# Mixture-of-experts stage of a small language model: gathered rows turned by TensorE, inner product turned by DMA, down product three tiles behind

## The reference

```python
h = tok(x)                                   # softmax of 4 coefficients, times 4 base rows
h = h + attn(layernorm(h))                   # 16 heads, q = k = v
xn = layernorm(h)
topk_logits, topk_idx = top_k(xn @ moe_router, 2)            # 8 experts, 2 for each token
w = softmax(topk_logits)
# for each (token, expert) pair, pairs sorted by expert:
gate, up = split(xn[token] @ moe_w13[expert])                # 256 -> 2 x 512
hidden = silu(gate) * up                                     # 512
h = h + sum over a token's two experts of w * (hidden @ moe_w2[expert])   # 512 -> 256
```

## Time and profile before

| | |
|---|---|
| Median of three runs | 920.97 us (919.45 to 924.36) |
| Profiled execution, its own time | 920.03 us |
| Its span | 918.3 us |
| TensorE busy with matmuls (PE) | 780.5 us, 85% |
| VectorE / ScalarE / GpSimd busy | 532.2 / 547.2 / 357.3 us |
| Expert stage | from 596.5 us to the end |
| TensorE in that stage, from 640 to 700 us | 59.66 of 60 us, granted clock 1.00 |
| DMA engines there | busy half of the time |

### The profile page before, as it was taken

The page is one execution under the profiler, slowest core; times in us unless marked ns, Lnnn a source line. Parts: engine busy times, 40 slices in busy tenths (PEclk is TensorE's granted clock), DMA queues, the critical chain, the costliest instruction groups (busy, mean ns, idle before and its releaser), DMA issues. The chain is left out here.

```text
span 918.3 us, 17297 instructions
## 1 busy us (share of the span) xinstructions
PE 780.5 (85%) x5470; PEld 331.6 (36%) x5521; DVE 532.2 (58%) x1617; ACT 547.2 (60%) x512; POOL 357.3 (39%) x311
## 2 busy tenths in 40 slices
PE   3499995988899889988988893079999999999994
PEld 2132221222222222222222221036666666666662
DVE  6734573647776657585646467725555555555552
ACT  0368994999999999999999993112222222222221
POOL 7660030320432133223320345335656556665652
PEclk9999997999999999999999996579999999999997
DMA  1030104012101110111011204035544455554442
GB/s 38 1 90 2 35 12 35 13 44 61 47 13 36 47 47 13 58 47 47 14 36 46 70 26 133 18 73 88 96 92 84 93 91 90 87 97 86 87 71 30
DMA packets 71920, 50.38 MB, mean 55 GB/s; under 512 B 45382, under 2 KB 67544, under 8 KB 71854
## 3 DMA queue, kind: packets, MB, share of 16 engines
q1 hardware_dynamic: 55598, 32.02, 14.7%
q0 software_dynamic: 16256, 17.55, 11.4%
HBM read 22.79 MB, written 17.57 MB: 44 GB/s over the span
## 5 line engine op out<-in xcount | busy, mean ns | idle before, releaser
L701 ACT ACTIVATE shared<-PS 128x1536 f32<-128x1536 f32 x342 | 467.9, 1472 | 55.1 <-PE PS L335 44.9
L347 PE MATMUL PS<-shared,va 128*32 128x512 f32 x2048 | 277.8, 615 | 3.4 <-DVE room L1141 3.1
L586 POOL DMA_INDIRECT slots<-pair_no,room x64 | 63.5, 992 | 382.8 <-DVE room L827 368.2
L1361 PE MATMUL PS<-w_p,room 128*128 x793 | 190.1, 382 | 15.0 <-DMA room<-room 12.9
L335 PE MATMUL PS<-room,ak 32*128 32x512 bf16 x1024 | 131.5, 391 | 53.2 <-ACT shared L701 44.7
L1409 ACT ACTIVATE room<-PS 128x512 f32<-128x512 f32 x69 | 41.3, 598 | 162.7 <-PE PS L1361 162.7
L1331 POOL DMA_INDIRECT out<-room,idx_tok x68 | 107.5, 1581 | 77.4 <-ACT room L1414 65.0
L1461 DVE CAST room<-PS 128x512 bf16<-128x512 f32 x68 | 47.0, 692 | 126.5 <-PE PS L1370 126.5
L1361 PEld LDWEIGHTS PS<-w_p,room 128*128 128x128 f16 x828 | 81.3, 98 | 99.2 <-issue 18.0
L335 PEld LDWEIGHTS PS<-room,ak 32*128 32x128 bf16 x1024 | 31.7, 91 | 205.1 <-ACT shared L701 150.0
L1378 PE MATMUL PS<-shared,room 128*128 x828 | 101.8, 273 | 0.3 <-DVE room L1463 0.3
(11 more groups left out here) (260 smaller groups left out, 650.4 us busy)
## 6 DMA issues: line engine op xcount, KB each, us to landing
room<-w SPq DMA_DIRECT2D x24, 512.0 KB, 4.8
xrows<-room SPq DMA_DIRECT2D x16, 258.0 KB, 3.1
out<-room SPq DMA_DIRECT2D x16, 256.0 KB
room<-xrows,idx_tok POOLq DMA_INDIRECT x70, 2.9
room<-room SPq DMA_TRANSPOSE x70, 3.5
out<-room,idx_tok POOLq DMA_INDIRECT x68, 4.1
slots<-pair_no,room POOLq DMA_INDIRECT x64, 6.8
xT<-xT SPq DMA_DIRECT2D x3, 256.0 KB, 5.9
```

The costliest lines, as they stand in the source:

```text
L347: last = pe.matmul(PS[32 * slot:32 * slot + 32, ACC, :], g.va[:, KT * (grp // HG) + kt, c, :], prob[:, (4 * quad + slot) % (RING * WIDE), ...
L586: pool.indirect_dma_start(g.slots, bass.IndirectOffsetOnAxis(pos_i[:, grp % 2, 2 * k + kk:2 * k + kk + 1].bitcast(U32), 0), g.pair_no[:, t ...
L701: act.activation(prob[:, at:at + n, :].rearrange("p n q -> p (n q)"), PS[:, buf:buf + n, :].rearrange("p c q -> p (c q)"), ACT.Exp).then_i ...
L1361: last = pe.matmul(PS[:, up_bank(k) + half, :], xsT[:, k, 2 * a + c, :], g.w13_p[:, w, c, ds(e, 1), FF * half:FF * half + FF].rearrange("p ...
```

## The change

Only the expert block changes, and one constant for it (`identh`, a float16 identity, written by one more VectorE instruction at the very start).

- The gathered rows are turned by TensorE (`turn_x`): four float16 transposes of 128 x 128 into the first half of bank 0 or bank 5, and one copy by ScalarE to `xsT` (`copy_x`).
- The inner product `hid` isn't turned by TensorE. VectorE splits it in place into two bfloat16 halves, L1441 and L1443 (now from SBUF to SBUF), and SyncE issues one DMA transpose of 128 x 1024 values, eight blocks, straight to `hidT`, which has four buffers now.
- In TensorE's program a step is `turn_x` of tile j + 4, `up` of tile j + 3, `down` of tile j.
- `act_s` and `hid` have one buffer each; the loop's last iteration is written out, 68 tiles are gathered and multiplied, and no 69th.
- GpSimd scatters tile j - 7 behind the gather of tile j, where it was tile j - 6.

```diff
@@ sync
-            sp.wait_ge(xs_in[k], arrived)
-            sp.sem_inc(x_landed, 1)
-            sp.dma_start_transpose(xsT[:, k], xs[:, k, 0:4 * P]).then_inc(xT_in[k], 16)
+            sp.wait_ge(hid_split, j + 1)
+            sp.sem_inc(sp_step, 1)
+            sp.dma_start_transpose(hidT[:, k], halves[:, k].rearrange("p a f -> p (a f)")).then_inc(hT_in[k], 16)
@@ gpsimd
-            for j in range(XBUF, tiles + 2):
+            for j in range(XBUF, tiles):
                 pool.wait_ge(weighed, j - XBUF + 1)
                 pool.wait_ge(up_mm, j - XBUF + 1)
                 gather(j)
-                if j >= XBUF + 2:
-                    scatter(j - XBUF - 2, apart)
+                if j >= XBUF + 3:
+                    scatter(j - XBUF - 3, apart)
@@ tensor
+        def turn_x(k, j, round_):
+            pe.wait_ge(xs_in[k], 16 * round_ + 16)
+            pe.wait_ge(xT_copied, j + 1)
+            for c in range(4):
+                last = pe.transpose(PS[:, XB[k % 2], 0:2 * P].bitcast(F16)[:, P * c:P * c + P], xs[:, k, P * c:P * c + P], g.identh[:])
+            last.then_inc(x_turned, 1)
+
+        def up(k, j, round_):
+            e = expert(j)
+            pe.wait_ge(xT_copied, j + 1 + FREE)
+            pe.wait_ge(hid_ready, j + 1)
...
-        def turn_hidden(k, ready, free):
-            pe.wait_ge(hid_ready, ready)
-            pe.wait_ge(hidT_ready, free)
-            for c in range(4):
-                last = pe.transpose(PS[:, HTB, P * c:P * c + P], hid[:, k, P * c:P * c + P], g.ident[:])
-            last.then_inc(hid_turned, 1)
...
+        def down(k, j, round_):
+            e = expert(j)
+            pe.wait_ge(hT_in[k], 16 * round_ + 16)
+            pe.wait_ge(y_copied, j + 1)
...
-                up((k + 1) % XBUF, expert(j + 2), i * 16 + 16 * ((k + 1) // XBUF + 1), j + FREE)
-                turn_hidden(k % 2, j + 1 + FREE, j + FREE)
-                down((k + 1) % 2, expert(j), j + FREE, j - 1 + FREE)
+                if not last:
+                    turn_x(k, j + XBUF, i + 1)
+                if not last or k == 0:
+                    up((k + 3) % XBUF, j + 3, i + (k + 3) // XBUF)
+                down(k, j, i)
+
+        for j in range(XBUF):
+            turn_x(j, j, 0)
+            if j >= 1:
+                up(j - 1, j - 1, 0)
+        steps(pe, body)
@@ scalar
+        def copy_x(k, j):
+            act.wait_ge(x_turned, j + 1)
+            act.copy(xsT[:, k].rearrange("p c q -> p (c q)"), PS[:, XB[k % 2], 0:2 * P].bitcast(F16)).then_inc(xT_copied, 1)
...
+                if not last:
+                    copy_x(k, j + XBUF)
+                if not last or k == 0:
+                    silu((k + 3) % XBUF, j + 3)
+                copy_y(k, j)
@@ vector
+            dve.wait_ge(hid_ready, j + 1 + FREE)
+            dve.tensor_copy(halves[:, k, 0], hid[:]).then_inc(split_step, 1)
+            dve.wait_ge(split_step, j + 1)
+            dve.tensor_tensor(halves[:, k, 1], hid[:], halves[:, k, 0], ALU.subtract).then_inc(hid_split, 1)
```

More of the change, by code:

```diff
@@ L1281, in up_bank, with steps @@
+    y_mm, y_copied, y_free = sem("y_mm"), sem("y_copied"), sem("y_free")
+    weighed = sem("weighed")
+    x_turned, xT_copied = sem("x_turned"), sem("x_copied")
+    XB = (0, 5)
+    YB = (6, 7)
     def up_bank(k):
         return 1 + 2 * (k % 2)
-    def steps(eng, body, end):
+    def steps(eng, body):
         more = eng.value_load(g.more[0:1, 0:1], min_val=0, max_val=1)
-        with eng.Fori(0, USUAL // XBUF) as i:
-            body(i)
+        with eng.Fori(0, USUAL // XBUF - 1) as i:
+            body(i, False)
@@ L1302, in body, with turn_hidden @@
-        def body(i):
-            for k in range(XBUF):
[L1304 to L1311, removed]
+        def turn_hidden(k, j):
+            sp.wait_ge(hid_split, j + 1)
+            sp.sem_inc(sp_step, 1)
+            sp.dma_start_transpose(hidT[:, k], halves[:, k].rearrange("p a f -> p (a f)")).then_inc(hT_in[k], 16)
+        def body(i, last):
+            for k in range(XBUF):
+                turn_hidden(k, i * XBUF + k)
@@ L1340, in run @@
                 gather(j)
-                if j >= XBUF + 2:
-                    scatter(j - XBUF - 2, apart)
-            for m in range(tiles - XBUF, tiles):
+                if j >= XBUF + 3:
+                    scatter(j - XBUF - 3, apart)
+            for m in range(tiles - XBUF - 3, tiles):
                 scatter(m, apart)
@@ L1354, in tensor, with expert @@
     def tensor(pe):
[L1355 to L1357 removed]
+        def expert(j):
+            col = j + 1
+            return pe.value_load(g.tile_expert[0:1, ds(col, 1) if not isinstance(col, int) else slice(col, col + 1)],
+                                 min_val=0, max_val=E - 1)
+        def turn_x(k, j, round_):
[8 more added lines that the diff above has]
+            pe.wait_ge(hid_ready, j + 1)
             for half in range(2):
@@ L1381, in down, with body @@
             last.then_inc(y_mm, 1)
[L1383 to L1388, removed]
-        pe.sem_inc(y_mm, FREE)
-        pe.wait_ge(zeroed, 2)
-        up(0, expert(1), 16, FREE)
-        def body(i):
+        def body(i, last):
             for k in range(XBUF):
                 j = i * XBUF + k
-                up((k + 1) % XBUF, expert(j + 2), i * 16 + 16 * ((k + 1) // XBUF + 1), j + FREE)
-                turn_hidden(k % 2, j + 1 + FREE, j + FREE)
-                down((k + 1) % 2, expert(j), j + FREE, j - 1 + FREE)
@@ L1400, in end @@
-        def end(tiles):
-            down(1, expert(tiles), tiles + FREE, tiles - 1 + FREE)
-        steps(pe, body, end)
-    def scalar(act):
-        def silu(k, up_done, free):
-            act.wait_ge(up_mm, up_done)
-            act.wait_ge(hid_ready, free)
-            act.activation(act_s[:, k, :], PS[:, up_bank(k), :], ACT.Silu).then_inc(silu_done, 1)
-        def copy_y(k, ready, free):
-            act.wait_ge(y_mm, ready)
-            act.wait_ge(y_free, free)
+                if not last:
+                    turn_x(k, j + XBUF, i + 1)
@@ L1414, in copy_y, with body @@
             act.copy(y_s[:, k, :], PS[:, YB[k % 2], 0:D]).then_inc(y_copied, 1)
         act.sem_inc(y_copied, FREE)
-        silu(0, 1, FREE)
-        def body(i):
+        act.sem_inc(xT_copied, FREE)
+        for j in range(XBUF):
+            copy_x(j, j)
+            if j >= 1:
+                silu(j - 1, j - 1)
+        def body(i, last):
             for k in range(XBUF):
                 j = i * XBUF + k
-                silu((k + 1) % 2, j + 2, j + FREE)
-                copy_y((k + XBUF - 1) % XBUF, j + 1 + FREE, j + 1)
@@ L1467, in end @@
-        def end(tiles):
-            pass
-        steps(dve, body, end)
+        steps(dve, body)
     return sync, gpsimd, vector, scalar, tensor
```

81 lines of the change are left out of this document (33 added, 48 removed).

## The result

No gain. The kernel after takes 923.5 us (median of 20 runs, 921.52 to 926.17), the kernel before on the same chip 921.03 (20 runs, 919.34 to 924.36): a ratio of 1.0026, 95% interval 1.0016 to 1.0036. Forecast were 907 us and a range of 900 to 915. The profiled execution took 925.23 us, its span 923.1.

A forecast was written before the change was run, and what follows sets the result against it. TensorE was taken as the bound, its sequencer just hidden. First up at 602.2, plus start, sixteen iterations of 16.8 us, last up and a 9.2 us end put the last scatter at 893.3, 13.9 us earlier: 907 us, range 900 to 915.

The forecast's parts named there:

- Start of the first up: Start of the expert stage: second tile turned on TensorE first, so up starts near 602.2 us instead of 603.28.
- To the start of the loop: Ahead of the loop: first up 4.7 us at the low clock, then two more pairs of turning and up, 5.6 us.
- Sixteen iterations: The loop of four tiles an iteration: 16.8 us each, the pace of TensorE's sequencer, 268.8 us in all.
- Last up and its way out: Behind the loop on TensorE: last up product 2.6 us and 0.2 for its way out, ending at 884.1 us.
- Its end to the last scatter: Last tile's way in the open after the last up: 9.2 us, between 8.3 and 10.5; before it was 4.8.
- step (1): Turning in the loop: cheaper transposes cut the array to 4.13 us a tile; the sequencer's 16.8 us an iteration becomes the pace.
- for every fourth: TensorE's loop before the change: 0.14 us more on every fourth tile, put down to the loop's branch.
- the rival in which the sequencer is hidden: In the loop the sequencer isn't the bound: 16.5 us an iteration, 902 us; chance 0.18.
- the sequencer loses more at the new seams: In the loop, load behind only 0.23 us of turning: iteration back to 17.4 us, 916.6 us; no-gain chance 0.16.
- The transposes don't keep pace: Eight-block DMA transposes in the loop set the period, TensorE waits in each down: 935 or 1098 us; chance 0.07.
- The gap forecast ahead of the last down: At the end TensorE stands still some 2.4 us; at half clock the last down takes 1.3 us more.
- the turning: Four transposes a tile on TensorE: 0.23 us in float16 instead of 0.44 in float32.

The follow-up runs named there:

- experiment 2: Changed kernel, with SyncE holding each DMA transpose until the down product of two tiles before is copied: 917.19 us, ratio 0.9892 to the kernel before.
- Experiment 8: Changed kernel, usual last four tiles right behind the loop, DMA transposes held back except in the last iteration: 903.06 us, ratio 0.9818 to the kernel before.
- experiment 4: Changed kernel, with the expert's number for up loaded ahead of the four turning transposes: 932.49 us, ratio 1.0049 to the kernel before.
- Experiment 5: Changed kernel, transposing only the upper halves (four blocks) and using them twice, so the lower halves are left out of the result: 917.01 us, one run.
- experiment 3: Changed kernel, usual last four tiles right behind the loop and every DMA transpose held back: 914.78 us, ratio 0.9851 to the kernel before.
- experiment 1: Changed kernel, with the usual last four tiles placed right behind the loop, ahead of the four extra tiles: 925.58 us, ratio 0.9975 to the kernel before.

## Why the prediction was wrong

The sum had the last scatter start at 893.3 us; it started at 912.23, 18.9 later. By its own terms:

| Term | Forecast | Measured | Difference |
|---|---|---|---|
| Start of the first up | 602.2 | 603.25 | +1.05 |
| To the start of the loop | 4.7 + 5.6 | 10.72 | +0.42 |
| Sixteen iterations | 16 x 16.8 = 268.8 | 277.8 | +9.0 |
| Idle ahead of the last up | 0 | 4.56 | +4.56 |
| Last up and its way out | 2.8 | 5.3 | +2.5 |
| Its end to the last scatter | 9.2 | 10.62 | +1.42 |

(The loop runs from the turning at 613.97 us to the end of its last down product, 1.31 us behind the start at 890.44.)

- **The pace, step (1), failed.** "Nothing that it issues has gone: the same two loads, as many waits, as many products", and therefore 4.0 us for a tile. The count was right and the durations weren't. The 0.57 us load behind the loop's branch and the 0.62 maximum were taken for the branch's effect and left at that; nobody asked what ran beside them. The trace of before had the answer: from 640 to 880 us 8 of 111 loads took over 0.32 us, each with a transpose's packets on 34 to 68% of the engines' time, where no quick one had over 17%. For the load of the earlier trace rows, 659.55 to 660.12 us:

```profile
q1 hardware_dynamic: 277, 0.07, 62.1%
```

  The 0.14 us "for every fourth" was misread for the same reason. Of 54 spacings of up products in that stretch 50 are 4.34 us and only four longer, 4.40 to 4.51, each with such a load in it. Behind the other branches there is no gap.

  The eight-block transposes were costed on DMA engines (68%, measured 69%) and by their landing (up to 8 us allowed, 3.9 measured), and by neither measure did they matter. What mattered was when they ran, beside which instruction of another engine's sequencer. Read with quick loads, the account of the sequencer was close: 4 x 4.133 = 16.5 us with the loop's branch in it (experiment 2), where 16.8 was forecast, and 16.5 is the array's time as well. So the two are level, the change has no slack for a longer load, and each 0.1 us of one goes straight into the pace. Experiment 8, without the collision, lands at 903 us, beside the 902 of the rival in which the sequencer is hidden (neither has the far branch in it). The rival "the sequencer loses more at the new seams" had the size right, 17.4 us an iteration (measured 277.8 / 16 = 17.36), and the reason wrong: not the 0.23 us of cover, as experiment 4 shows.
- **"The transposes don't keep pace" was the wrong mechanism for the right suspect.** No down product in the loop waited for one.
- **The end failed by a term that wasn't there.** The sum had a written-out last iteration and no price for getting into it. The order of the two `If` blocks could be read in the code, and the branch of before took only 0.345 us; the jump over four extra tiles' code takes 4.2 us, and the gap takes TensorE's clock for the next up, 2.7 us more. The gap forecast ahead of the last down came too, 1.92 us for 2.4, and cost less clock than I had put there (1.80 us instead of 1.47). The 1.4 us more of the end come from GpSimd: the chain ends on the landing of a scatter, 4.09 us from 906.15, before the last two can go, and 2.4 us pass from the last copy's end (909.86) to the last scatter, where before it was 0.8. In the loop that landing was rightly costed at nothing; at the end four down products come close together, and it isn't.
- **The start was mis-sized a little.** Up stood 5.7 us behind the first gather in the forecast and 5.2 in the trace; the whole stage began 1.5 us later in this execution.
- **Right:** the turning, 0.23 us of array time; 68 silus and scatters; the array's 4.13 us; nothing to pay in the loop for the gathers, GpSimd or VectorE.
- **A slip in the chances:** as stated they add up to 0.82 for faster and 0.10 for slower, not 0.83 and 0.09.

Counted from the first gather, the last scatter starts 314.2 us later in the kernel after (598.06 to 912.23) and 310.7 in the one before (596.53 to 907.24). The 69th up product (2.6 us) and the quicker start (1.6) did arrive. The pace, which should have brought some 9 us, brought none, the open end costs what was foreseen and 1.4 more, and the branch with its clock takes 7.1: a gain of 13.9 us at the last scatter has become a loss of 3.5.

## What to carry to other kernels

When TensorE is busy nine tenths and more, cost its sequencer like an engine of its own: list register loads, waits and branches of a period with their durations, and look what else runs beside each load before you move a DMA transpose. Two kernels with the same busy time can be bound by different things, and the starts of the products tell them apart, the busy column doesn't. And where code for a rare case stands between a loop and its common continuation, the common case pays for the jump; put it next to the loop. A wait that is good in the steady state belongs out of the last iteration.

## What the hardware did that I had not expected

- A register load from SBUF (TENSOR_LOAD, 0.30 us) took up to 0.66 us beside the packets of a DMA transpose. In the kernel after this told slow and quick loads apart without exception; elsewhere it doesn't. Experiment 5 has slow loads beside a scatter's packets alone, and in experiments 2, 3, 5 and 8 some were quick beside a full q1, begun less than 0.8 us before its last packet. A gather's packets never did it: over the nine traces with such loads 123 of them had gather packets on more than half of the engines in their first 0.3 us, and none took over 0.32. The three kinds differ in size (256 bytes, 1 KB and 4 KB) and in more than that, and what holds a load up stays open: that moving the transposes away cures it is shown, the mechanism isn't. ScalarE's silu, which runs beside the slow loads too, isn't the cause: in experiment 2, 53 loads of 0.30 us have it beside them.
- A branch cost TensorE's sequencer 0.07 to 0.08 us where the program went on in the code right behind, 0.34 over some code, and 3.3 to 5.4 us over a lot of it. At which distance it jumps up was not measured.
- VectorE's cast from SBUF to SBUF, forecast at 0.43 us from the earlier trace rows, took 0.59 us on the mean of the stage. The one of the 68 with no GpSimd instruction beside it, the last, took 0.43; whether that is the reason wasn't tested. VectorE had room for it. The group of the page, part 5:

```profile
L1441 DVE CAST room<-shared 128x512 bf16<-128x512 f32 x68 | 40.0, 589 | 2.3
```

- A DMA transpose of eight blocks landed in 3.9 us (median), where four landed in 3.5. The Trainium skill's page "VectorE: DVE Perf Modes", section "The three transpose paths", has 1309 ns for one block; eight of them at that price would be 10.5 us, and the trace contradicts it as a price per block within one instruction.
- The last transpose of a run, with little work left on the chip to hide it, took 4.6 us to land in experiment 8 and 4.1 in experiment 1; in the kernel after the last down product started 3.4 us behind the end of the split. A pipeline that ends in a DMA has that as its tail.
